# A gated attention and feed-forward layer on one core: the prologue's loads, splits and projections reordered

## The reference

```python
q = (layernorm(x) @ Wq.T + bq)   # heads of 32 features
k = (ctx @ Wk.T + bk)
v = (ctx @ Wv.T + bv)
scores = einsum('bhqd,bhkd->bhqk', q, k) * 32 ** -0.5   # masked, causal
x = x + tanh(g_xattn) * (softmax(scores) @ v @ Wo.T + bo)

n = layernorm(x); p = n shifted by one token
r = sigmoid((mu_r * n + (1 - mu_r) * p) @ W_r.T)
h = square(relu((mu_k * n + (1 - mu_k) * p) @ W_k.T))
x = x + tanh(g_ffn) * r * (h @ W_v.T)
```

## Time and profile before

| | us |
|---|---|
| median of 3 runs | 1967.93 |
| lowest and highest | 1967.72 to 1968.57 |
| the profiled execution, its own time | 1967.85 |
| its span, first to last instruction | 1966.1 |
| PE busy in it | 1905.0 (97%) |
| DVE, ACT and POOL busy | 1357.3, 1089.3, 1092.2 |
| mean granted TensorE clock | 0.992 |

### The profile page before, as it was taken

How to read it: one execution, slowest core, us unless ns; L and a number is a source line. 1 busy time by engine, 2 the same in 40 slices (tenths; PEclk the granted TensorE clock), 3 DMA queues, 4 the chain that set the end, 5 groups by cost and what they waited for, 6 DMA issues and landing times.

```text
span 1966.1 us, 35998 instructions
## 1 busy us (share of the span) xinstructions
PE 1905.0 (97%) x11648; PEld 1494.7 (76%) x11648; DVE 1357.3 (69%) x3528; ACT 1089.3 (55%) x2059; POOL 1092.2 (56%) x1745
## 2 busy tenths in 40 slices
PE   4899999999999999999999999998989999999999
PEld 3677777777777777777777777776768888888887
DVE  4777677777677777777777677777566575756654
ACT  4555555455555555555555555555565665656562
POOL 4566656666566666666666576666633333434331
PEclk9999999999999999999999999999999999999999
DMA  6544554545446444554545545454133223132311
GB/s 189 118 113 122 136 143 108 141 111 135 116 124 156 119 118 121 132 149 109 134 116 135 125 111 154 119 139 122 66 107 108 86 81 113 70 106 83 107 65 64
DMA packets 128697, 229.71 MB, mean 117 GB/s; under 512 B 18656, under 2 KB 20704, under 8 KB 127616
## 3 DMA queue, kind: packets, MB, share of 16 engines
q1 hardware_dynamic: 128512, 227.43, 43.2%
HBM read 92.06 MB, written 33.59 MB: 64 GB/s over the span
## 4 chain that ended last, share of the span: by engine, by line
PE 81%; DVE 12%; issue 3%; ACT 2%; POOL 1%; DMA 1%; SPq 0%; ACTq 0%; DVEq 0%; POOLq 0%
PE proj_ps L41 13%; PE proj_ps L42 12%; PE proj_ps L43 12%; PE value_ps L1274 8%; PE score_ps L1231 7%; PE prob_ps L1255 5%; DVE score_ps L961 4%; PE score_ps L41 3%; PE score_ps L42 3%; PE score_ps L43 3%; DVE split_max L971 2%; PE sum_ps L1282 2%; PE sum_ps L43 1%; PE value_ps L43 1%; PE sum_ps L41 1%
## 5 line engine op out<-in xcount | busy, mean ns | idle before, releaser
L961 DVE CUSTOM_DVE_ANT_0 score_ps<-score_ps,causal 128x128 f32<-128x128 f32 (+3 forms) x1024 | 487.6, 504 | 276.1 <-PE score_ps L1231 275.2
L616 ACT ACTIVATE probs<-prob_ps 128x512 f32<-128x512 f32 (+1 forms) x768 | 394.7, 528 | 393.9 <-PE sum_ps L1285 201.2
L1231 PE MATMUL score_ps<-k_stack,q_stack 97*128 97x128 f32 (+3 forms) x1024 | 317.6, 351 | 9.3 <-DVE least L961 5.4
L1255 PE MATMUL prob_ps<-q_stack,k_stack 100*128 100x512 f32 (+3 forms) x1024 | 281.5, 315 | 1.3 <-ACT probs L616 1.2
L451 POOL TENSOR_TENSOR prob_sum<-probs 128x384 f32<-128x384 f32 x256 | 259.8, 1015 | 0.0
L440 POOL TENSOR_SCALAR_AFFINE_SELECT probs<-probs 128x256 f32<-128x256 f32 x256 | 105.2, 411 | 250.9 <-ACT probs L616 250.9
L1231 PEld LDWEIGHTS score_ps<-k_stack,q_stack 97*128 97x128 f32 x1024 | 187.6, 189 | 56.7 <-issue 14.1
L497 POOL TENSOR_TENSOR kact<-square,kact 128x512 fp32r<-128x512 f32 x64 | 84.1, 1325 | 236.9 <-ACT kact L692 236.9
L454 POOL TENSOR_TENSOR prob_sum<-prob_sum,probs 128x256 f32<-128x256 f32 x256 | 190.3, 743 | 37.6 <-POOL prob_sum L451 1.3
L1255 PEld LDWEIGHTS prob_ps<-q_stack,k_stack 100*128 100x128 f32 x1024 | 191.9, 191 | 20.1 <-DMA q_stack<-max_rows 1.8
L444 POOL TENSOR_SCALAR_AFFINE_SELECT probs<-probs 128x256 f32<-128x256 f32 x256 | 107.1, 418 | 159.8 <-ACT probs L616 159.8
(11 more groups left out here) (146 smaller groups left out, 4821.6 us busy)
## 6 DMA issues: line engine op xcount, KB each, us to landing
k_stack<-staged SPq DMA_DIRECT2D x384, 128.0 KB
q_stack<-staged SPq DMA_DIRECT2D x384, 128.0 KB, 3.1
tiles<-in_x SPq DMA_DIRECT2D x16, 1024.0 KB, 5.5
x_io<-in_x SPq DMA_DIRECT2D x16, 1024.0 KB, 7.8
x<-x_io SPq DMA_DIRECT2D x64, 256.0 KB, 2.9
res<-x SPq DMA_DIRECT2D x64, 256.0 KB, 3.4
out_x<-res SPq DMA_DIRECT2D x64, 256.0 KB, 2.0
tiles<-in_ctxT SPq DMA_DIRECT2D x60, 256.0 KB, 3.1
```

The lines of the kernel that those rows point to most:

```text
L616: nc.scalar.activation(probs[:, u % RING, lo:hi], prob_ps[(3 * u + c) % 2][:, 0:hi - lo], ACT.Exp, scale=SCALE).then_inc(exp_done, 1)
L961: nc.vector.tensor_tensor_reduce(out=here, in0=here, in1=causal[:, LATE - P * t:S], scale=-1.0, scalar=3e38, op0=ALU.add, op1=ALU.min, acc ...
L1231: last = nc.tensor.matmul(here[:, at:at + P * (t + 1)], q_stack[n][0:MASK_ROW + 1, j, P * t:P * t + P], k_stack[n][0:MASK_ROW + 1, j, 0:P ...
L1255: last = nc.tensor.matmul(here[:, at:at + width], k_stack[n][0:ROWS, j, P * k:P * k + P], q_stack[n][0:ROWS, j, P * k:S], start=True, stop ...
```

## The change

Only the prologue and the split of the output weight are altered; the slots are the same otherwise.

- **SP.** The mask comes first, then x in four DMAs of 256 KB, then context and k's weight in turn, a k-step (256 KB) of each, on semaphores of their own. Then the biases, q's weight, v's weight; then, behind a wait for POOL's scaled mask, the mask's bias, and only now the two gates. `stack_k(0)` and `stack_k(2)` follow, then the feed-forward's mixing vectors, the output's weight and bias, and `stack_q(0)` and `stack_q(2)`.
- **ACT and DVE** split context and k's weight step by step, and the other weights in four pieces each. ACT applies the layer norm between the copies of the transposed x. The copy of `ident_parts`, the gates' tanh and the table load go behind the split of v's weight. The wait for `gate_loaded` at the head of ACT's stream stays where it was, and a second one stands ahead of the tanh.
- **PE** projects k, step by step, then does all four transposes, q, both blocks of v, and two k-steps of q's second group. `FIRST` loses three exceptions, so v's block 0 waits until q has left its bank.
- **POOL** scales the mask and sets one stack's rows ahead of the inverse deviations, and the three others behind them.
- **The output's weight** is subtracted in two slots, two pieces in each, not in one piece in slot 1.

```diff
-        FIRST = {"k0": None, "x0": None, "v0": ("x0", 0), "x2": ("v0", 0), "q1": ("q0", 0)}
+        FIRST = {"k0": None, "x0": None}
...
-            load_x(0)
+            sp.dma_start(x_io[0:B, 0, :].bitcast(I32), mask).then_inc(mask_loaded, 16)
+            for m in range(T):
+                sp.dma_start(tiles[:, m, :], x[0, P * m:P * m + P]).then_inc(x_first_loaded[m], 16)
+            for k in range(K):
+                sp.dma_start(c_raw[:, k, :], ctxT[0, P * k:P * k + P]).then_inc(c_first_loaded[k], 16)
+                sp.dma_start(w_raw["k"][:, k, :], wkT[:, k, :]).then_inc(wk_first_loaded[k], 16)
+            for n, col in enumerate((bq, bk, bv)):
+                sp.dma_start(columns[:, n, :], col).then_inc(columns_loaded, 16)
+            sp.dma_start(w_raw["q"], wqT).then_inc(w_loaded["q"], 16)
+            sp.dma_start(w_raw["v"], wvT).then_inc(w_loaded["v"], 16)
+            sp.wait_ge(mask_scaled, 1)
+            sp.dma_start(mask_bias, x_io[0:B, 1, :]).then_inc(mask_stored, 16)
             sp.dma_start(gate[:], g_xattn.partition_broadcast(P)).then_inc(gate_loaded, 16)
             sp.dma_start(ffn_gate[:, 0:1], g_ffn.partition_broadcast(P)).then_inc(ffn_gate_loaded, 16)
...
+            stack_k(0)
+            stack_k(2)
...
             sp.dma_start(w_raw["o"], woT).then_inc(w_loaded["o"], 16)
             sp.dma_start(bo_gated[:], bo.partition_broadcast(P)).then_inc(bo_loaded, 16)
...
-            stack_k(0)
             stack_q(0)
-            stack_k(2)
             stack_q(2)
...
             def split_weights(name):
                 act.wait_ge(w_loaded[name], 16)
-                nc.scalar.copy(w[name][0][:], w_raw[name]).then_inc(w_high, 1)
+                for k in range(K):
+                    nc.scalar.copy(w[name][0][:, k, :], w_raw[name][:, k, :]).then_inc(w_high[name], 1)
...
             act.wait_ge(gate_loaded, 16)
+            for k in range(K):
+                act.wait_ge(c_first_loaded[k], 16)
+                nc.scalar.copy(cT[0][:, k, :], c_raw[:, k, :]).then_inc(c_high, 1)
+                act.wait_ge(wk_first_loaded[k], 16)
+                nc.scalar.copy(w["k"][0][:, k, :], w_raw["k"][:, k, :]).then_inc(w_high["k"], 1)
+            for m in range(T):
+                apply_layernorm(0, m)
+                if m > 0:
+                    high_part_x(0, m - 1)
+            high_part_x(0, T - 1)
+            act.wait_ge(columns_loaded, 16 * 3)
+            high_part_k(0, 0)
+            split_weights("q")
             act.wait_ge(pool_const, 5)
             nc.scalar.copy(ident_parts[:], ident[:]).then_inc(ident_ready, 1)
+            high_part_q(0, 0)
+            split_weights("v")
+            act.wait_ge(gate_loaded, 16)
             nc.scalar.activation(gate[:], gate[:], ACT.Tanh).then_inc(gate_ready, 1)
...
-                if i == 1:
-                    split_weights(3, "o")
+                if i in (1, 2):
+                    for k in range(2):
+                        split_weights("o", 2 * (i - 1) + k)
...
+            for k in range(K):
+                dve.wait_ge(c_high, k + 1)
+                nc.vector.tensor_tensor(cT[1][:, k, :], c_raw[:, k, :], cT[0][:, k, :].bitcast(F32), ALU.subtract).then_inc(c_low, 1)
+                split_weights("k", k)
+            for m in range(T):
+                low_part_x(0, m)
             low_part_k(0, 0)
-            split_weights(2, "q")
-            low_part_x(0, 2)
-            low_part_x(0, 3)
+            for k in range(K):
+                split_weights("q", k)
             low_part_q(0, 0)
+            for k in range(K):
+                split_weights("v", k)
...
             pe.wait_ge(pool_const, 5)
-            pe.wait_ge(ident_ready, 1)
             for k in range(K):
                 project_k(0, 0, k)
-            transpose_x(0, 0)
-            transpose_x(0, 1)
-            for k in range(K):
-                project_v(0, 0, k)
-            transpose_x(0, 2)
-            transpose_x(0, 3)
-            for k in range(K):
-                project_v(0, 1, k)
+            for m in range(T):
+                transpose_x(0, m)
             for k in range(K):
                 project_q(0, 0, k)
+            for m in range(2):
+                for k in range(K):
+                    project_v(0, m, k)
+            pe.wait_ge(ident_ready, 1)
```

More of the change, by code:

```diff
@@ L147, in gated_layer @@
         sum_ps = psum("sum_ps")
-        w_loaded = {n: sem(f"w{n}_loaded") for n in "qkvo"}
-        w_high, w_low = sem("w_high"), sem("w_low")
+        w_loaded = {n: sem(f"w{n}_loaded") for n in "qvo"}
+        w_high, w_low = ({n: sem(f"w{n}_{part}") for n in "qkvo"} for part in ("high", "low"))
         ffn_loaded = {n: sem(f"ffn_w{n}_loaded") for n in "krv"}
@@ L162, in gated_layer @@
         xt_done, xt_high, xt_low = sem("xt_done"), sem("xt_high"), sem("xt_low")
-        c_raw_loaded = sem("c_raw_loaded")
+        x_first_loaded = [sem(f"x_first_loaded{m}") for m in range(T)]
+        c_first_loaded = [sem(f"c_first_loaded{k}") for k in range(K)]
+        wk_first_loaded = [sem(f"wk_first_loaded{k}") for k in range(K)]
         c_loaded = [sem(f"c_loaded{k}") for k in range(K)]
@@ L525, in _ @@
                                     pattern=[[-1, P]], channel_multiplier=1).then_inc(pool_const, 1)
-            invert_deviations(0)
-            pool.wait_ge(ln_step, NORM_STEPS)
-            for n, rows in enumerate(q_stack + k_stack):
-                nc.gpsimd.memset(rows[MASK_ROW:P].bitcast(F32), 1.0).then_inc(stacks_set, 1)
-                pool.wait_ge(stacks_set, n + 1)
             pool.wait_ge(mask_loaded, 16)
@@ L533, in _ @@
                                     ALU.mult).then_inc(mask_scaled, 1)
+            pool.wait_ge(pool_const, 5)
+            pool.wait_ge(mask_scaled, 1)
+            nc.gpsimd.memset(k_stack[0][MASK_ROW:P].bitcast(F32), 1.0).then_inc(stacks_set, 1)
+            pool.wait_ge(stacks_set, 1)
+            invert_deviations(0)
+            pool.wait_ge(ln_step, NORM_STEPS)
+            for n, rows in enumerate((q_stack[0], k_stack[1], q_stack[1])):
+                nc.gpsimd.memset(rows[MASK_ROW:P].bitcast(F32), 1.0).then_inc(stacks_set, 1)
+                pool.wait_ge(stacks_set, n + 2)
             pool.wait_ge(gate_ready, 1)
@@ L824, in _ @@
             nc.scalar.preload_act_table_set("natural_log_exp_and_others")
-            act.wait_ge(c_raw_loaded, 16)
-            nc.scalar.copy(cT[0][:], c_raw).then_inc(c_high, K)
-            split_weights("k")
-            for m in range(T):
-                apply_layernorm(0, m)
-            split_weights("v")
-            high_part_x(0, 0)
-            high_part_x(0, 1)
-            act.wait_ge(columns_loaded, 16 * 3)
-            high_part_k(0, 0)
-            split_weights("q")
             copy_v(0, 0)
-            high_part_x(0, 2)
-            high_part_x(0, 3)
             copy_v(0, 1)
-            high_part_q(0, 0)
             for i in SLOTS:
@@ L925, in layernorm_stats @@
             def layernorm_stats(b, m):
-                dve.wait_ge(x_loaded, 16 * (b + 1))
+                if b == 0:
+                    dve.wait_ge(x_first_loaded[m], 16)
+                else:
+                    dve.wait_ge(x_loaded, 16 * b)
                 wait(dve, ln_stats, T * b)
@@ L1225, in scores @@
                     pe.wait_ge(k_stacked[n][j // 2], k_stack_count(G))
+                if c == 0 and u in (0, HG):
+                    pe.wait_ge(stacks_set, (2, 4)[G])
                 if u > 0 or c == 2:
@@ L1300, in project_q @@
                     pe.wait_ge(xt_low, T * (b + 1))
-                    pe.wait_ge(w_low, 3)
+                if b == 0 and g == 0:
+                    pe.wait_ge(w_low["q"], k + 1)
                 last = exact_product(nc, bank(f"q{g}")[:], lambda k: [part[:, k, P * g:P * g + P] for part in w["q"]],
@@ L1311, in project_k @@
                     pe.wait_ge(c_low, K * b + k + 1)
-                    pe.wait_ge(w_low, 1)
+                if b == 0 and g == 0:
+                    pe.wait_ge(w_low["k"], k + 1)
                 last = exact_product(nc, bank(f"k{g}")[:], lambda k: [part[:, k, P * g:P * g + P] for part in w["k"]],
@@ L1322, in project_v @@
                     pe.wait_ge(c_low, K * (b + 1))
-                    pe.wait_ge(w_low, 2)
+                if b == 0 and m == 0:
+                    pe.wait_ge(w_low["v"], k + 1)
                 last = exact_product(nc, bank(f"v{m}")[:], lambda k: [part[:, k, P * m:P * m + P] for part in cT],
```

26 lines of the change are left out of this document (6 added, 20 removed).

## The result

| | before | changed |
|---|---|---|
| median, us | 1966.88 (12 runs) | 1970.46 (12 runs) |
| lowest to highest | 1965.35 to 1968.57 | 1967.45 to 1973.16 |
| ratio to before, 95% interval | | 1.0018 (1.0010 to 1.0026) |
| profiled execution, own time | 1967.85 | 1971.44 |
| its first scores, first probabilities | 41.19, 55.07 | 47.26, 58.58 |

The account below looks back on a forecast made before the run. PE, busy 97% of the span, was taken as the bound, so a prologue edit shifts the whole run. Scores 4.8 us later, minus 1.6 and 0.2 in the first slots, gave + 3.0, hence 1970.9 us; range 1966.0 to 1974.5.

Parts of the forecast that it names:

- The gate's wait, G: Head of ACT's stream: the first copy waits for the gate's DMA, landing at 18.3 us, bounds 17.0 to 20.3.
- the 5 MB: Loads ahead of the gate on SP's queue, ending with v's weight; forecast to have landed at 17.1 us, 19.0 before.
- the hole: DMA engines move nothing between 6.0 and 6.5 us in the kernel before, because of the gates; costs up to 2.8 us.
- From G to PE's chain: Prologue steps from the gate's landing through k, layer norm, transposes, q and v; scores 27.7 us after the landing.
- The low clock in q: PE's clock assumed low during q's matmuls, 0.43 us each; a clock that stayed up would bring the scores to 45.3.
- PE's chain is the later one: Ahead of the first scores: PE's matmuls end at 46.0 us, 0.7 later than q's stack lands through SP's queue, 45.3.
- The first slots: Behind the first scores: 1.6 us back from PE's full clock, 0.2 from the output's weight in pieces.
- The sum: Whole kernel: + 4.8 for later scores, - 1.6 for the clock, - 0.2 for the output's weight, + 3.0 us in all.
- The gate did not overtake the weights: Rival on SP's queue: the gate lands ahead of the weights, ACT starts by 13.3, time 1965.9 us; chance 0.14.
- that rival: Queue ahead of q's first stack: the stack lands at 48.9, PE idles 2.9 us, time 1975.4 us; chance 0.21.
- As described: Rival at ACT's head: the gate's wait does not bind, scores come 6.5 us earlier, time 1959.6 us; chance 0.04.

Follow-up runs that it names:

- experiment 3: The changed kernel with the output's weight subtracted in one instruction in slot 1, as before the change; 1971.91 us, ratio 1.0025 to the kernel before.
- experiment 9: The kernel before with eleven unused matmuls of 128x512 between q's second group and the first scores; 1968.66 us, ratio 1.0004.
- experiment 8: Experiment 7's kernel with mixing vectors and output's weight and bias issued ahead of all stacks, q's first stack ahead of the second k stack; ratio 0.9968.
- experiment 1: The changed kernel without ACT's wait for the gate at the head of its stream; 1962.86 us, ratio 0.9979 to the kernel before.
- experiment 5: The changed kernel with context and k's weight each loaded by one DMA, head wait kept; 1971.18 us, ratio 1.0021 to the kernel before.
- experiment 6: The changed kernel without the head wait, DVE's splits of context and k's weight held back until POOL has the inverse deviations; 1965.27 us, ratio 0.9984.
- experiment 7: The changed kernel without the head wait, with 16 unused matmuls while PE waits for the transposed x; 1962.77 us, ratio 0.9976.
- experiment 4: The kernel before with both gates issued behind q's weight, tanh and table load moved ahead of q's staging, no head wait; 1970.59 us, ratio 1.0020.
- experiment 2: The changed kernel with the head wait kept, but both gates' DMAs issued right behind x; 1965.12 us, ratio 0.9989 to the kernel before.
- experiment 11: Experiment 8's kernel with six more unused matmuls ahead of v's block 0; 1961.05 us, ratio 0.9960 to the kernel before.
- experiment 12: Experiment 11's kernel with context and k's weight loaded by one DMA each; 1963.94 us, ratio 0.9978 to the kernel before.

## Why the prediction was right

By its own steps, read at the profiled executions:

- **The gate's wait, G.** Forecast 18.3, measured 19.3. The order of service was right. Inside the term two errors stand against each other: v's weight, the end of the 5 MB, landed at 19.0 and not at the 17.1 of my sum, and the gate came 0.3 behind it and not 1.15. So the 2.8 us of the hole that I took off did not come back here. The pieces moved at 211 to 256 GB/s for three microseconds, which is part of it; but the same loads had the gate at 18.34 in experiment 3, and how much of the 1.0 is the pieces stays open.
- **From G to PE's chain.** q's first matmul was forecast at G + 13.45 and came at G + 13.25, its last at G + 18.1 (37.41 - 19.33 = 18.08), v at G + 20.8 (20.96), the scores at G + 27.7 (27.93). The low clock in q, which I had to assume, was there: one matmul each 0.43.
- **PE's chain is the later one.** By hardly anything, not by 0.7 us. q's stack was issued at 39.58 (forecast 40.0), as soon as DVE had staged q (38.80 + 0.75), since SP had reached it at 39.2; but the copies that the scores need landed only at about 47.2, where I had 45.3: the weight load ahead of the scores stood 0.33 us for them. The stack's landing was mis-sized by 1.9 us, and it cost nothing because PE's chain was 1.2 later than forecast too. Had the stack alone been that late, the scores would have waited. That is luck.
- **The first slots.** Forecast: 1.6 for the clock and 0.2 for the output's weight. From the scores to the probabilities it took 13.88 us before and 11.32 after, 2.56 less. Experiment 3 gives 1.0 of these to the pieces of the output's weight: I had taken 0.2 of a possible 1.0, since I read a weight load's wait for the maxima as the next bound, and it was not one. The other 1.56 I had ascribed to the clock, and that the number fits is luck: experiment 9 has the clock alone, and nothing is gained in the end. What the changed kernel has besides is its second k stack and both q stacks issued before slot 0. Their order is not what counts: experiment 8 has the order of the kernel before and takes 11.26, but its second q stack is issued at 33.06, 4.7 us ahead of the scores, where the kernel before had 41.16 and 41.19. That the full clock and this head start together make the 1.56 fits the numbers; no run gave the kernel before the head start alone.
- **The sum.** + 6.07 for the scores (forecast 4.8), - 2.56 behind them (forecast 1.8), + 3.5 at the probabilities, + 3.6 at the end (forecast 3.0). Two errors, of 1.3 and 0.8 us, had opposite signs, so the total is nearer than its parts; that too is luck. What was right is the path: ACT's wait for the gate sets the start, PE's chain follows it, and less than half of the delay is given back.
- **Rivals.** The gate did not overtake the weights (it landed 0.3 behind v's). q's stack landed with PE's arrival and not later, nearer to that rival than I had it. "As described" was refuted by the trace, and experiment 1 shows what it would have been: I had worked out 8.3 us below the kernel before, with the scores at 34.7; it is 4.1 below by the ratio, with the scores at 39.54. Two things were missing in it: ACT's last piece of k's weight was there only at 13.30 and not at 11.3, and DVE's subtractions stretch POOL's steps, which no step of mine had.
- **The clock as noise.** The changed kernel's runs spread over 5.7 us. Its profiled execution has a low stretch between 70 and 80 us, that of the kernel before one between 90 and 100. Which wait triggers a fall differs from run to run. That this makes the spread is argued, not shown.

## What to carry to other kernels

Before moving a load back in a queue, look for every engine that waits for it ahead of other work: a wait at the head of an in-order stream turns the smallest copy into the start of everything. Draw all chains to the point that counts, the issuing queue's too, and read each as an offset from the event that starts them; such offsets held in the changed kernel to 0.3 us where absolute times were off by 1, as long as the clock was the one assumed (in experiment 5, with another clock under q and v, the scores came at G + 28.6 and not + 27.9). And a wait of PE may cost more than its own length, by a lower clock behind it, at a place where the change did nothing: 1.6 to 1.8 us behind a wait of 2.3 in experiments 6 to 8. A profiled execution that gains or loses as much has to be checked for that first.

## What the runs showed of the hardware

- **DVE's subtraction of two float32 tensors in SBUF blocks POOL's steps.** A step of 128x4 elements lasts 0.20 us alone, 0.55 to 0.75 beside pieces of 128x512, 2.12 to 2.36 beside 128x2048. ACT's copies of the same tensors don't do this (experiment 6).
- **Two copies of 4 bytes to each of 128 partitions leave the DMA engines all but idle** where they stand between large ones (share 0.03 in the earlier trace rows); behind v's weight the first of them cost 0.3 us.
- **DMAs of 256 KB in turn from two tensors** moved 211 to 256 GB/s at a DMA share of 0.84 to 0.93 between 7 and 10 us, and 235 to 307 as a mean over these three in the seven kernels that have them and the gates late; with one of 1 MB each it was 405, 428 and 435. That the last of the loads lands later by it is not shown.
- **The granted clock** went to 0.50 behind waits of PE of 1.97 us (experiment 9), 2.89 and 4.23 (experiment 4). It does not do so each time. PE waits 2.25 or 2.26 us ahead of v in eight kernels: from there to the scores the mean clock was 1.00 in the changed kernel and in experiments 1 and 3, and 0.80 or 0.81 in experiments 2, 5, 6, 7 and 8. With six more matmuls in that wait, so that 0.90 was left of it (experiments 11 and 12), it was 1.00.
